# Last node stage of a graph kernel: residual and statistics one unit ahead, and one table load

## The reference

```python
x = _layernorm(x + _L0_gnn_ref(x, edge_index, edge_weight, W1, b1, W2, b2), axis=-1)
x = _layernorm(x + _L1_gnn_ref(x, edge_index, edge_weight, edge_attr_50, ...), axis=-1)

def _layernorm(x, axis=-1, eps=1e-05):
    m = jnp.mean(x, axis=axis, keepdims=True)
    v = jnp.var(x, axis=axis, keepdims=True)
    return (x - m) / jnp.sqrt(v + eps)
```

## Time and profile before

| | |
|---|---|
| median of 3 runs | 8774.11 us (8772.1 to 8775.9) |
| the profiled execution, its own time | 8796.3 us |
| its span, first to last instruction | 8794.7 us |
| `layer1_nodes` in it, from the first load issued to the end of the span | 8693.20 to 8794.7 us |
| first `y` to the end of the last `norm` | 8696.17 to 8789.06 us |

### The profile page before, as it was taken

The page is one execution under the profiler, slowest core; times in us unless marked ns, Lnnn a source line. Parts: engine busy times, 40 slices in busy tenths (PEclk is TensorE's granted clock), DMA queues, the critical chain, the costliest instruction groups (busy, mean ns, idle before and its releaser), DMA issues. The chain is left out here.

```text
span 8794.7 us, 201979 instructions
## 1 busy us (share of the span) xinstructions
PE 5927.9 (67%) x35386; PEld 4731.0 (54%) x35658; DVE 5851.1 (67%) x17865; ACT 3465.1 (39%) x6782; POOL 6213.8 (71%) x6560
## 2 busy tenths in 40 slices
PE   5676676667676676666655556666767666666787
PEld 3444444444444444444444445666666666666676
DVE  6666666666666666665655556777777777777776
ACT  3434344443444444444544443334444343443302
POOL 6777777777777777775377777777777777777710
PEclk7766676666776767667755557888888888888897
DMA  5444454444444445444444446666666666666676
GB/s 165 154 152 153 150 155 151 154 151 152 154 153 153 153 153 153 153 153 148 143 133 134 135 131 191 212 213 213 213 215 213 212 215 211 215 215 211 215 238 203
DMA packets 805506, 1537.47 MB, mean 175 GB/s; under 512 B 193406, under 2 KB 207156, under 8 KB 804963
## 3 DMA queue, kind: packets, MB, share of 16 engines
q1 hardware_dynamic: 595415, 1097.64, 38.8%
q0 software_dynamic: 209712, 436.16, 16.9%
q10 hardware_dynamic: 348, 3.33, 0.1%
HBM read 971.97 MB, written 564.58 MB: 175 GB/s over the span
## 5 line engine op out<-in xcount | busy, mean ns | idle before, releaser
L1353 POOL DMA_INDIRECT sorted_messages<-rows,sidx x3224 | 3115.5, 966 | 1153.4 <-issue 946.9
L516 POOL DMA_INDIRECT xg<-x_rows,gidx x3224 | 3050.4, 946 | 1032.8 <-issue 858.9
L584 PE MATMUL bank<-attr,nn 128*128 128x512 f32 x1612 | 1484.7, 1075 | 191.0 <-DMA attr<-attr_cols 181.6
L573 PE MATMUL bank<-onehot,xg 128*128 128x42 f32 x6448 | 945.1, 303 | 845.5 <-DMA xg<-x_rows,gidx 838.1
L1281 PE MATMUL bank<-hot,block_rows 128*128 128x128 f32 x8256 | 1390.0, 344 | 30.0 <-DVE hot L1435 29.9
L1281 PEld LDWEIGHTS bank<-hot,block_rows 128*128 128x128 f32 x8256 | 1342.8, 258 | 55.7 <-issue 17.8
L573 PEld LDWEIGHTS bank<-onehot,xg 128*128 128x128 f32 x6448 | 877.1, 212 | 882.0 <-DMA xg<-x_rows,gidx 874.4
L1251 PE MATMUL bank<-w_nn2T,e_hid 128*128 128x128 f32 x6448 | 1041.9, 314 | 293.1 <-DMA e_hid<-hidden 285.2
L1251 PEld LDWEIGHTS bank<-w_nn2T,e_hid 128*128 128x128 f32 x6448 | 1008.2, 226 | 250.3 <-DMA e_hid<-hidden 217.2
L465 ACT ACTIVATE soft<-bank 128x512 f32<-128x512 f32 x808 | 475.3, 588 | 1332.8 <-PE bank L584 1332.5
L1262 PE MATMUL bank<-h1w,ohT 128*128 128x128 bf16 x3224 | 337.9, 268 | 982.1 <-DVE ohT L1382 982.1
(11 more groups left out here) (220 smaller groups left out, 8235.4 us busy)
## 6 DMA issues: line engine op xcount, KB each, us to landing
block_rows<-sorted_messages SPq DMA_DIRECT2D x346, 792.0 KB
hidden<-hid SPq DMA_DIRECT2D x404, 512.0 KB
e_hid<-hidden SPq DMA_DIRECT2D x403, 512.0 KB
sorted_messages<-zero SPq DMA_DIRECT2D x403, 264.0 KB
dstb<-dst SPq DMA_DIRECT2D x403, 256.0 KB
attr<-attr_cols SPq DMA_DIRECT2D x403, 204.0 KB
xg<-x_rows,gidx POOLq DMA_INDIRECT x3224
sorted_messages<-rows,sidx POOLq DMA_INDIRECT x3224
```

What stands on the lines that cost most here:

```text
L516: pool.indirect_dma_start(xg[b][s][:, :], None, x_rows, bass.IndirectOffsetOnAxis(ap=gidx[b][s // HALF][:, s % HALF:s % HALF + 1], axis=0) ...
L573: nc.tensor.matmul(bank[0][:, 0:WIN], xg[b][s][:, :], onehot[:, s, :], start=(s == 0), stop=(s == SUB - 1)).then_inc(summed[b], 1)
L584: nc.tensor.matmul(bank[2 + h][:, :], nn1[:, :], attr[:, h, :], start=True, stop=True).then_inc(z1_set, 1)
L1353: pool.indirect_dma_start(table, bass.IndirectOffsetOnAxis(ap=sidx[b][h][:, s:s + 1], axis=0), rows[b][h][:, s, :], None).then_inc(landed[ ...
```

## The change

It is in `layer1_nodes` alone. `residual` with its statistics is called one unit ahead on DVE, and so is `root` on ACT: where the list of DVE was residual(u), factors(u), it is now residual(u + 1), factors(u), and that of ACT is root(u + 1), norm(u). The count `steps` is split in two, `steps` (9 per unit, for the residual and the statistics) and `factor_steps` (2 per unit); SP, PE and `root` wait on the first, `norm` on the second. ACT gets one explicit load of its table set ahead of the stage.

```diff
--- before.py
+++ after.py
@@ -1471,6 +1471,19 @@
                     add_turn(tail_slot(r, k), lambda u: hot_block(tail_slot(turn, buffer), buffer, u, tail_landing(turn, buffer)))
 
 
+STAT_STEPS, FACTOR_STEPS = 1 + 2 * G, 2
+
+
+def stat_step(c, h, k):
+
+    return STAT_STEPS * (2 * c + h + 2) + k
+
+
+def factor_step(c, h, k):
+
+    return FACTOR_STEPS * (2 * c + h + 2) + k
+
+
 def layer1_nodes(nc, sem, sbuf, x1_d, aggT, lin2T, bias3, ones3, ident, eps, zero, spare, bank, out):
 
     f32 = mybir.dt.float32
@@ -1482,7 +1495,7 @@
 
     lin, std_set = sem("f_lin"), sem("f_std")
     o_set, passed_act = sem("f_o"), sem("f_passed_act")
-    steps, passed = (sem(f"f_{n}") for n in ("steps", "passed"))
+    steps, factor_steps, passed = (sem(f"f_{n}") for n in ("steps", "factor_steps", "passed"))
     x1_in, stored = ([sem(f"f_{n}{k}") for k in range(2)] for n in ("x1_in", "stored"))
 
     def node_rows(dram, c, h):
@@ -1494,7 +1507,7 @@
         def _(sp):
             def load_x1(c, h):
                 k = h % 2
-                sp.wait_ge(steps, ln_step(c, h - 2, Y_SET))
+                sp.wait_ge(steps, stat_step(c, h - 2, 1))
                 sp.dma_start(x1[k][:, :, :], node_rows(x1_d, c, h)).then_inc(x1_in[k], 16)
 
             in_turn(sp, (1, load_x1))
@@ -1503,7 +1516,7 @@
         def _(pe):
             def linear(u):
                 k = u % 2
-                pe.wait_ge(steps, ln_step(0, u - 2, Y_SET))
+                pe.wait_ge(steps, stat_step(0, u - 2, 1))
                 nc.tensor.matmul(bank[2 + k][:, :], ones3[:, :], bias3["lin2b"][:, :], start=True, stop=False)
                 for g in range(G):
                     at = u * UNIT + g * P
@@ -1519,20 +1532,21 @@
         def _(act):
             def root(c, h):
                 k = h % 2
-                act.wait_ge(steps, ln_step(c, h, VAR_SET))
+                act.wait_ge(steps, stat_step(c, h, STAT_STEPS))
                 nc.scalar.activation(std[k][:, :], mean_var[k][:, :, 1], ACT.Sqrt, bias=eps[:, 0:1]).then_inc(std_set, 1)
 
             def norm(c, h):
                 k = h % 2
-                act.wait_ge(steps, ln_step(c, h, LN_DONE))
+                act.wait_ge(factor_steps, factor_step(c, h, FACTOR_STEPS))
                 wait_apart(act, stored[k], 16 * (c + h // 2 + 1), passed_act)
                 for g in range(G):
                     nc.scalar.activation(o[k][:, g, :], y[k][:, g, :], ACT.Identity,
                                          bias=shift[k][:, g:g + 1], scale=rstd[k][:, g:g + 1]).then_inc(o_set, 1)
 
+            nc.scalar.preload_act_table_set("sqrt_and_others")
             act.sem_inc(std_set, CREDIT)
             act.sem_inc(o_set, 2 * G)
-            in_turn(act, (0, root), (0, norm))
+            in_turn(act, (1, root), (0, norm))
 
         @block.gpsimd
         def _(pool):
@@ -1556,16 +1570,25 @@
                 dve.wait_ge(x1_in[k], 16 * (c + h // 2 + 1))
                 dve.tensor_tensor(y[k][:, :, :], bank[2 + k][:, :].rearrange("p (g d) -> p g d", g=G),
                                   x1[k][:, :, :], ALU.add).then_inc(steps, 1)
-                layer_norm_stats(dve, steps, passed, c, h, y[k], stats[k], mean_var[k])
+                wait_apart(dve, steps, stat_step(c, h, 1), passed)
+                for g in range(G):
+                    dve.bn_stats(stats[k][:, g, :], y[k][:, g, :]).then_inc(steps, 1)
+                wait_apart(dve, steps, stat_step(c, h, 1 + G), passed)
+                for g in range(G):
+                    dve.bn_aggr(mean_var[k][:, g, :], stats[k][:, g, :]).then_inc(steps, 1)
 
             def factors(c, h):
                 k = h % 2
                 dve.wait_ge(std_set, done(c, h))
                 wait_apart(dve, o_set, rows_freed(c, h), passed)
-                layer_norm_factors(dve, steps, passed, c, h, mean_var[k], std[k], rstd[k], shift[k])
-
-            dve.sem_inc(steps, 2 * LN_STEPS)
-            in_turn(dve, (0, residual), (0, factors))
+                dve.reciprocal(rstd[k][:, :], std[k][:, :]).then_inc(factor_steps, 1)
+                wait_apart(dve, factor_steps, factor_step(c, h, 1), passed)
+                dve.scalar_tensor_tensor(shift[k][:, :], mean_var[k][:, :, 0], -1.0, rstd[k][:, :],
+                                         ALU.mult, ALU.mult).then_inc(factor_steps, 1)
+
+            dve.sem_inc(steps, 2 * STAT_STEPS)
+            dve.sem_inc(factor_steps, 2 * FACTOR_STEPS)
+            in_turn(dve, (1, residual), (0, factors))
 
 
 _OUTS = [((NPAD, D), "float32")]
```

## The result

The change makes the kernel slower: median 8795.03 us (9 runs, 8789.09 to 8799.29) against 8774.11 us (9 runs, 8768.73 to 8776.01). The ratio is 1.0026 with a 95% interval of 1.0015 to 1.0036, so 13 to 32 us. The forecast was 27.1 us and 8801.2 us; the time lies in the range given.

The account below looks back on a forecast made before the run. No engine is full; in the stage DVE and ACT take turns. Round terms sum to 4.84 us a unit, where it was 3.72, ending the stage 27.1 us later: 8774.1 + 27.1 = 8801.2 us, range 8792 to 8812.

Parts of the forecast that it names:

- The closed round: In layer1_nodes, residual(u + 1) waits for norm(u - 1) and holds up factors(u): 4.84 us a unit, where it was 3.72.
- the gap from the statistics to the reciprocal: Term of the round on DVE, end of statistics to reciprocal: 0.06 us, bounds 0 and 0.15.
- from reciprocal to shift: Term of the round on DVE, start to start: 0.32 us.
- residual(1): Second residual of the stage, needs no norm: forecast to start at 8698.70, after a gap of 0.28 us.
- from norm to residual: Term of the round, end of norm on ACT to residual on DVE: 0.22 us, bounds 0.17 and 0.44.
- The sum's own lower bound: All terms of the round at their lower bounds: 4.70 us a unit instead of 4.84, total 8798 us.
- The forecast for the profiled execution: The profiled execution, 8796.3 us before, should take 8823.4 us, with the first residual starting at 8696.17 as before.
- Edits that cost nothing: ACT's root, PE's products, transfers, stores and split counts stay hidden; the ten loads' 3.4 us saving would not be missed.
- Rival A: Not slower: the wait on finished rows doesn't bind, DVE's own 3.07 us a unit sets the pace, 8759.9 us; 5%.
- Rival B: Slower by less than 0.2%: round over 0.4 us shorter than summed, or 10 us given back outside the stage; 3%.
- Rival C: Table loads dearer than the turns show: all 12.8 us of them on top, a further 9.4 us off, 8791.8 us; 2%.
- the estimate of 3.9 us slower: Ten loads priced by the skill's page give back 26.6 us instead of 3.4: 27.1 + 3.4 - 26.6 = 3.9 us slower.

Follow-up runs that it names:

- e4: The change with units written out and a third y tile, against the kernel before: stage 70.9 us, time 8754.92 us, ratio 0.9979; repeated: 71.0 us, 8755.35 us.
- e3: The change with its 25 units written out instead of a loop, still two y tiles: stage 111.2 us, against 116.6 for the change.
- e2: The change with a table load kept ahead of each even unit's root, 12 loads in the stage: stage 116.6 us, as in the change.
- e7: The change with the new order on DVE alone, ACT in the old order: stage 117.6 us, against 116.6 for the change.
- e8: The change with the new order on ACT alone, DVE in the old order: stage 108.9 us, against 116.6 for the change.
- e5: The change with one more activation at the head of each norm: stage 128.9 us, against 116.6 for the change.
- e6: e1 with one more activation at the head of each norm: stage 88.9 us, against 88.4.
- e1: The change with the old order back, one table load and split counts kept: stage 88.4 us; 8768.55 us against 8772.87 for the kernel before, ratio 0.9995.

## Why the prediction was right

- **The closed round** was the main step and is shown. It is there in the timeline with its wait 23 times at 2.03 us (forecast some 23 times about 2.0). It opens with a third tile (e4 against e3) and stays with everything else that was tried: with the loads kept (e2), with the new order on one engine alone (e7, e8), written out (e3, 4.43 us a unit). And it pays in full for a longer norm (e5), which the old order does not (e6).
- **Its size** came out 3.4 us too large: 27.1 forecast, 23.7 in the stage; 20.9 by the medians, whose interval holds both. The terms that were too large are small. The main one is the gap from the statistics to the reciprocal, put at 0.06 and measured at 0.01 in one unit (8684.87 to 8684.88) and -0.09 in the other, for there the reciprocal starts ahead of the end of the aggregate at 8689.68. That is 0.10 a unit over 23 units, 2.3 us. I had taken 0 as the lower bound of this gap, and so excluded an overlap without a reason. Further -0.015 from reciprocal to shift, 0.3 us, and residual(1) came 0.17 earlier; the rest is hundredths in the other terms and one short unit, 4.43 us, at the loop's end. The other terms held: 0.21 for 0.22 from norm to residual, 2.24 for 2.25, 1.65 for 1.65. The units of a turn took 4.81 and 4.62 us, and not 4.84 both.
- **The lower end was close.** The sum's own lower bound was 23.9 us more in the stage and 8798 us; the stage gave 23.7, just below it, for the gap that went under its bound, and the median of 8795.03 lies 3 us below. Most of these 3 us are the medians, which show 20.9 where the stage shows 23.7, and the range had allowed some 3 us for that. The forecast for the profiled execution, 8823.4 us, missed by about 29: it took the start of the stage as fixed, and the stage began 25.3 us earlier.
- **Edits that cost nothing**: right for the loads in the new order (e2), of which I had said that their saving would not be missed. Their worth in the old order was 4.5 us (e1) and not 3.4: each 0.4, not 0.34, and 0.4 once behind the loop, where one statistics instruction of the kernel before came late.
- **Rival A** (not slower, DVE's own work as the limit) was no way for this change, and is what e4 then showed as a kernel. I had priced it at 3.07 us a unit, in the loop; written out it is 2.58. **Rival B** (slower by less than 0.2%) didn't come: the stage's 23.7 us and the median's 20.9 are both over its 17.5, though the lower end of the interval, 13 us, is not. **Rival C** fell with e1 and e2: the ten loads were worth 4.5 us and not 12.8.
- The Trainium skill, "ScalarE: Activation LUTs", section "What ACT_TABLE_LOAD costs", counts some 2.66 us for a switch of sets. In e1 taking ten reloads away gave 4.5 us, and in e2 keeping them cost nothing; behind a reload of the set that is already active no drain shows here, the root starts 0.02 us after it. So the estimate of 3.9 us slower priced reloads by a figure that is for another case. No run here has a change between two sets inside this stage.

What stays open: in every written-out run each eighth unit takes 0.36 to 0.4 us longer (e4: the statistics at 8687.30 start 0.52 us after the residual, where that gap is 0.15 or less in other units; the profile names only the residual itself for it). I didn't test what it is.

## What to carry to other kernels

Before work is moved ahead by one unit, ask of each wait in it not only what it waits for but what now stands between it and its releaser, and what it holds up behind it on its engine. Here two tiles were enough for the old order, in which the residual runs beside the norm of the unit before. With the residual moved one more unit ahead, the wait for a free tile became the path, and only with a third tile was the order worth anything: written out, the order alone cost 27.9 us, the tile alone gave nothing, and both together gained 12.3. For a change of 0.2%, read the stage in the trace and not the total, since the start of the stage moved by up to 30 us between executions with the same code ahead of it.

## What the runs showed of the hardware that was not expected

- Where the chain shows two sequencer instructions of DVE between a norm's end and the residual it releases, the residual starts 0.21 us after that end (the change); where it shows none, 0.02 us after (e3).
- With nothing between them on DVE, the reciprocal starts 0.09 us before the aggregates ahead of it have ended, and takes 0.14 us instead of 0.18 (the change, one unit of each turn).
- The 1283 ns of a table load disappear in a longer wait of the same engine: with 1.19 us of waiting left behind each, twelve loads in the stage cost under 0.1 us (e2).
